# Graph layers in fp32: the states of 33 units transposed by VectorE in blocks and rearranged by DMAs through DRAM, where TensorE transposed them

## The chip, the cores and the metric

One core of one Trainium2 chip. The metric is the device time of one execution in microseconds. The engines are named as the profile names them: PE (TensorE), ACT (ScalarE), DVE (VectorE), POOL (GpSimd) and SP (SyncE, which here issues DMAs only).

## The reference

Four graph layers work on x of shape (16, 512, 128) with one matrix adj of shape (512, 512). Each layer's output is added to its input and normalised over the last axis:

```python
x = _layernorm(x + L0(x, adj, weight, bias))              # (adj @ x + x) @ W + b, rows scaled to length 1
x = _layernorm(x + L1(x, adj, adj, w3.., u3.., w5.., 5))  # gated recurrence, five steps
x = _layernorm(x + L2(x, adj, W, b))                      # degree-normalised adj @ x, then W
x = _layernorm(x + L3(x, adj, W, e, bias))                # attention over adj: self and neighbour parts
```

One step of the recurrence L1, on a state h of shape (16, 512, 128):

```python
m = einsum('nm,bmd->bnd', adj, h)                  # both matrices are adj here
u3 = h @ u3_w.T + u3_b
av = concatenate([m, m], -1)
z = sigmoid(av @ w3_w.T + w3_b + u3)
r = sigmoid(av @ w4_w.T + w4_b + u3)
hv = tanh(av @ w5_w.T + w5_b + (r * h @ u5_w.T + u5_b))
h = (1 - z) * h + z * hv
```

## The kernel before, in words

**Units and slots.** One batch element in one layer or one recurrent step is a unit, so there are 16 x 8 = 128: units 0 to 15 are the first layer, 16 to 95 the five steps, 96 to 111 the third layer and 112 to 127 the last. Every engine runs the same loop over slots `s` (`for s in range(SLOTS): slot(s)`). In slot s the unit s is aggregated and earlier units are at later stages. Nothing but the order of instructions in each engine's `slot` and semaphores sets the order; there is no planner.

**Layouts.** Node 4p + t stands on partition p. A product with adj contracts over the nodes, so it wants a state with nodes on partitions: `nat_hi` and `nat_lo`. The element-wise work and the products with weights want features on partitions: `feat`, 128 x 512 per batch element. What DVE makes of a step is `feat`; for the next step it must be turned into `nat_*`.

**Two parts.** Products run on operands of a rounded type (fp32r). To keep fp32 precision each operand X is split into a high part and a low part X - high, and a product is three matmuls: high x high, high x low, low x high. An aggregation (L1061 to L1067) is 12 matmuls of 512 columns: four chunks of nodes, three products each, `nat_*` as the stationary operand (loaded by LDWEIGHTS) and adj as the moving one.

**PE in a slot of the recurrence.** 12 matmuls of the aggregation of unit s; 3 for the reset state of s - 2 into `cand_ps` (L1072); for u = s - 1 the gate product into `gate_ps[u % 2]`, 6 matmuls (L1085, L1087), and 3 of the candidate (L1089); then the transposes of `turns_at(s)`, for a state 4 of 128 x 128 in fp32 into `turn_ps` (L1103); and last 3 matmuls that add the difference of the update and the reset gate's weights to the same bank `gate_ps[u % 2]` (L1142), before which PE waits for `r_made`, ACT's sigmoid reading that bank (L493).

**ACT in a slot.** `gate_z` of s - 2 (L458), `agg_hi` of s (L476), tanh into `cand` of s - 2 (L486), the sigmoid `gate_r` of s - 1 (L493), `feat_hi` (L503), `reset_hi` (L512), and `nat_hi` of the state s - 4 from `turn_ps` (L518). In the outer layers it also squares rows (L527), seeds biases (L536), normalises (L441) and makes `nat_hi` from `res` (L432, L463, L540).

**DVE in a slot.** `agg_lo` (L817), three operations that end in the new state `feat` of s - 2 (L822, L826, L829), `gate_r` times the state of s - 1 (L834), `feat_lo` (L838), `reset_lo` (L843), and `nat_lo` of the state s - 4 from `turn_ps` (L848). In the outer layers statistics (L863, L867), sums (L777, L782) and `nat_lo` from `res` (L696, L877) stand there too.

**POOL** works on statistics only: it has nothing in the middle of the recurrence. **SP** issues all DMAs from one queue in the order written: loads, two copies of adj's parts, reloads of `later` at slots about 36 and 46, small transfers, and the stores of the results. `cand[u % 2]` alternates by unit: ACT's tanh of u overwrites that of u - 2.

**When a state is turned.** A state unit u (16 to 79) is finished by DVE in slot u + 2, transposed in slot u + 4 (`STATE_LAG`), and used as `nat_*` by the aggregation of slot u + 16. Slots 88 and 93 are the two slots of the recurrence, once all its stages are filled, in which `turns_at` is empty.

Of the kernel before, what the change touches and what calls it, by code (L numbers as in the profile page):

```python
# [22 lines left out]
P = 128  # L23
B, N, D = 16, 512, 128
# [148 lines left out]


def flat(v):
    return v.rearrange("p a n -> p (a n)")


def graph_layers(nc, x, adj, w0, b0, w3, b3, u3, ub3, w4, b4, w5, b5, u5, ub5, w2, b2, wl3, e, bl3, mix_dram, d_dram, out):
    with ExitStack() as ctx:  # L180
        def sb(name, shape, dt=F32):
            return ctx.enter_context(nc.sbuf_tensor(name, shape, dt))
# [158 lines left out]
        def _(sp):  # L341
# [77 lines left out]
        def _(act):  # L419
# [3 lines left out]
            for t in range(T):  # L423
                if t == T - 1:
                    act.wait_ge(x_in[0], 16)
                    act.activation(nat_hi[:, 0, :, :], res[:, 0, :, :], ACT.Copy).then_inc(x_hi_made, 1)
                act.wait_ge(eye_turned, t + 1)
                act.activation(eye_hi[:, :, t * P:(t + 1) * P], prep_ps[t][:, :].rearrange("p (k i) -> p k i", k=T),
                               ACT.Copy).then_inc(eye_hi_made, 1)
            for b in range(1, 3):  # L430
                act.wait_ge(x_in[b], 16)
                act.activation(nat_hi[:, b, :, :], res[:, b, :, :], ACT.Copy).then_inc(x_hi_made, 1)  # L432

# [12 lines left out]
            def slot(s):  # L446
# [13 lines left out]
                for n in norms_at(s, "split"):  # L460
                    if stage(n) != L3:
                        wait_normed(act, n)
                        act.activation(nat_hi[:, n % B, :, :], res[:, n % B, :, :], ACT.Copy).then_inc(split_hi_made, 1)  # L463
                for n in norms_at(s, "back"):
# [48 lines left out]
                u = s - STATE_LAG  # L513
                if is_inner(u):
                    k = TURN_NO["state", u]
                    act.wait_ge(turned, k + 1)
                    act.wait_ge(agg_done, u + 1)
                    act.activation(nat_hi[:, u % B, :, :], turn_ps[k % 2][:, :].rearrange("p (t d) -> p t d", t=T),  # L518
                                   ACT.Copy).then_inc(state_hi_made, 1)
# [18 lines left out]
                if s + 3 < B:  # L538
                    act.wait_ge(x_in[s + 3], 16)
                    act.activation(nat_hi[:, s + 3, :, :], res[:, s + 3, :, :], ACT.Copy).then_inc(x_hi_made, 1)  # L540
                if s == ADJ_AT:
# [45 lines left out]
        def _(pool):  # L587
# [23 lines left out]
            def slot(s):  # L611
# [15 lines left out]
                for n in norms_at(s, "stats"):  # L627
# [33 lines left out]
        def _(dve):  # L661
# [32 lines left out]
            def x_lo(b):  # L694
                dve.wait_ge(x_hi_made, b + 1)
                dve.tensor_tensor(nat_lo[:, b, :, :], res[:, b, :, :], nat_hi[:, b, :, :].bitcast(F32),  # L696
                                  ALU.subtract).then_inc(x_lo_made, 1)
# [14 lines left out]
            def slot(s):  # L712
# [132 lines left out]
                u = s - STATE_LAG  # L845
                if is_inner(u):
                    dve.wait_ge(state_hi_made, u - B + 1)
                    dve.tensor_tensor(nat_lo[:, u % B, :, :],  # L848
                                      turn_ps[TURN_NO["state", u] % 2][:, :].rearrange("p (t d) -> p t d", t=T),
                                      nat_hi[:, u % B, :, :].bitcast(F32), ALU.subtract).then_inc(turn_read, 1)  # L850
                for n in norms_at(s, "stats"):
# [22 lines left out]
                for n in norms_at(s, "split"):  # L874
                    if stage(n) != L3:
                        dve.wait_ge(split_hi_made, nth(SPLIT, n))
                        dve.tensor_tensor(nat_lo[:, n % B, :, :], res[:, n % B, :, :],  # L877
                                          nat_hi[:, n % B, :, :].bitcast(F32), ALU.subtract).then_inc(split_lo_made, 1)
                if s + 3 < B:
# [65 lines left out]
        def _(pe):  # L945
# [82 lines left out]
            def slot(s):  # L1028

                if s < UNITS:  # L1030
                    if s < B:
                        if s:
                            pe.wait_ge(x_lo_made, s + 1)
                    elif 2 * B <= s < AFTER:
                        pe.wait_ge(turn_read, reads(TURN_NO["state", s - B]))
                    else:
                        pe.wait_ge(split_lo_made, nth(SPLIT, s - B))
# [10 lines left out]
                    if s == 0:  # L1048
                        pe.wait_ge(eye_lo_made, 1)
                        pe.wait_ge(eye_hi_made, T)  # L1050
                        pe.wait_ge(x_hi_made, 1)
                        for k in range(T):
                            pe.matmul(ps, nat_hi[:, b, k, :], m_hi[:, k, :], start=(k == 0), stop=False)
                        pe.wait_ge(x_lo_made, 1)
                        for k in range(T):
                            pe.matmul(ps, nat_lo[:, b, k, :], m_hi[:, k, :], start=False, stop=False)
                        pe.wait_ge(eye_lo_made, T)
                        for k in range(T):
                            last = pe.matmul(ps, nat_hi[:, b, k, :], m_lo[:, k, :], start=False, stop=(k == T - 1))
                    else:  # L1060
                        for k in range(T):  # L1061
                            if s == AFTER + B:
                                pe.wait_ge(turn_read, reads(TURN_NO["mix", k]))
                            pe.matmul(ps, nat_hi[:, b, k, :], m_hi[:, k, :], start=(k == 0), stop=False)  # L1064
                            pe.matmul(ps, nat_hi[:, b, k, :], m_lo[:, k, :], start=False, stop=False)  # L1065
                            last = pe.matmul(ps, nat_lo[:, b, k, :], m_hi[:, k, :], start=False, stop=(k == T - 1))  # L1066
                    last.then_inc(agg_done, 1)  # L1067
# [102 lines left out]
```

## Time and profile before

| | |
|---|---|
| median of 3 runs | 760.96 us (760.62 to 761.38) |
| profiled execution, time / span | 760.57 us / 758.7 us |
| granted clock of PE | 0.998 |
| busy: PE, PE weight load | 747.5 us (99%), 626.9 us (83%) |
| busy: DVE, ACT, POOL | 638.1 us (84%), 503.1 us (66%), 159.4 us (21%) |
| DMA | 11612 packets, 17.21 MB |

The span is what the profiler recorded from the first to the last instruction; the execution's own time is a little longer. Busy time counts overlapping instructions once. Matmuls are pipelined: a row's duration is longer than the step from one start to the next, so PE's pace is read from the starts in the timeline, and a PE that is busy all the time can still be held up. On ACT and DVE too the recorded durations overlap somewhat. "PEld" is the weight load of PE. L numbers are lines of the kernel.

### The profile page before, as it was taken

The numbers are of one execution on the slowest core, as the hardware profiler recorded it, in microseconds if no ns is written. First come the engines' busy times: TensorE is split into PE (matmuls) and PEld (weight loads), VectorE is DVE, ScalarE is ACT, GpSimd is POOL, SyncE is SP. The second block draws the span as 40 slices with busy tenths as digits, with TensorE's granted clock in tenths as the row PEclk, the third lists the DMA queues.
The fourth block names the chain that finished last, engine by engine and source line by source line (L and its number), as shares of the span: only waits on it lengthen the run. The fifth ranks groups of instructions, "written<-read, shape, count | busy, mean of one in ns | idle before, by whom it ended". The sixth has DMA issues, their size and how long they took to land.

```text
span 758.7 us, 11706 instructions
## 1 busy us (share of the span) xinstructions
PE 747.5 (99%) x3768; PEld 626.9 (83%) x3768; DVE 638.1 (84%) x1473; ACT 503.1 (66%) x1047; POOL 159.4 (21%) x307
## 2 busy tenths in 40 slices
PE   8999999999999999999999999999999999999996
PEld 7888788888888888888888888888888888788886
DVE  5899998888888998877777788777999999787775
ACT  4899777666666676666666666666587858864433
POOL 1878420000000000000000000000122257654333
PEclk9999999999999999999999999999999999999999
DMA  6500000000031001000000000000000000101112
GB/s 213 221 1 2 1 1 1 1 1 1 0 119 15 0 2 56 1 0 1 1 1 0 1 2 0 1 1 1 0 1 1 1 0 2 26 4 42 57 43 84
DMA packets 11612, 17.21 MB, mean 23 GB/s; under 512 B 4512, under 2 KB 6048, under 8 KB 10912
## 3 DMA queue, kind: packets, MB, share of 16 engines
q1 hardware_dynamic: 11552, 16.47, 6.5%
q8 instruction: 31, 0.51, 0.3%
q14 instruction: 29, 0.24, 0.1%
HBM read 9.12 MB, written 5.25 MB: 19 GB/s over the span
## 4 chain that ended last, share of the span: by engine, by line
PE 80%; DVE 9%; ACT 6%; POOL 2%; issue 2%; DMA 1%; SPq 0%; POOLq 0%; ACTq 0%; DVEq 0%
PE agg_ps L1064 12%; PE agg_ps L1066 12%; PE agg_ps L1065 12%; PE gate_ps L973 6%; PE gate_ps L975 6%; PE gate_ps L974 6%; PE cand_ps L973 4%; PE cand_ps L975 4%; PE cand_ps L974 4%; PE turn_ps L1103 4%; PE gate_ps L980 3%; PE cand_ps L980 3%; DVE stats L863 1%; ACT res L441 1%; PE turn_ps L1107 1%
## 5 line engine op out<-in xcount | busy, mean ns | idle before, releaser
L1064 PE MATMUL agg_ps<-adj_hi,nat_hi 128*128 128x512 f32 x384 | 152.1, 396 | 0.0
L1066 PE MATMUL agg_ps<-adj_hi,nat_lo 128*128 128x512 f32 x384 | 150.2, 391 | 0.0
L1065 PE MATMUL agg_ps<-adj_lo,nat_hi 128*128 128x512 f32 x384 | 149.6, 390 | 0.0
L642 POOL TENSOR_SCALAR shift<-mean_var 128x4 f32<-128x4 f32 x62 | 24.5, 396 | 408.8 <-DVE mean_var L867 406.7
L817 DVE TENSOR_TENSOR agg_lo<-agg_ps,agg_hi 128x512 fp32r<-128x512 f32 x80 | 55.1, 689 | 57.5 <-ACT agg_hi L476 57.5
L512 ACT ACTIVATE reset_hi<-gate_r 128x512 fp32r<-128x512 f32 x80 | 50.6, 633 | 78.1 <-DVE gate_r L834 78.1
L493 ACT ACTIVATE gate_r<-gate_ps,bias 128x512 f32<-128x512 f32 x80 | 55.2, 690 | 48.4 <-PE gate_ps L975 48.4
L1066 PEld LDWEIGHTS agg_ps<-adj_hi,nat_lo 128*128 128x128 f32 x384 | 72.1, 188 | 16.2
L1065 PEld LDWEIGHTS agg_ps<-adj_lo,nat_hi 128*128 128x128 f32 x384 | 72.2, 188 | 15.6
L1064 PEld LDWEIGHTS agg_ps<-adj_hi,nat_hi 128*128 128x128 f32 x384 | 72.1, 188 | 15.1
L476 ACT ACTIVATE agg_hi<-agg_ps 128x512 fp32r<-128x512 f32 x80 | 48.7, 608 | 44.0 <-PE agg_ps L1066 43.7
L644 POOL TENSOR_TENSOR rstd<-mean_var,half 128x4 f32<-128x4 f32 x62 | 69.2, 1116 | 5.2
L973 PE MATMUL gate_ps<-agg_hi,w_hi 128*128 128x512 f32 x160 | 69.5, 434 | 0.6 <-ACT gate_r L493 0.4
L975 PE MATMUL gate_ps<-agg_lo,w_hi 128*128 128x512 f32 x160 | 62.8, 393 | 0.0
L974 PE MATMUL gate_ps<-agg_hi,w_lo 128*128 128x512 f32 x160 | 62.7, 392 | 0.0
L843 DVE TENSOR_TENSOR reset_lo<-gate_r,reset_hi 128x512 fp32r<-128x512 f32 x80 | 55.4, 693 | 8.4 <-ACT reset_hi L512 0.7
L822 DVE TENSOR_TENSOR cand<-cand,feat 128x512 f32<-128x512 f32 x80 | 55.2, 690 | 4.6
L486 ACT ACTIVATE cand<-cand_ps,bias 128x512 f32<-128x512 f32 x80 | 55.2, 691 | 5.6
L826 DVE TENSOR_TENSOR cand<-cand,gate_z 128x512 f32<-128x512 f32 x80 | 55.4, 692 | 2.7
L829 DVE TENSOR_TENSOR feat<-feat,cand 128x512 f32<-128x512 f32 x80 | 55.3, 692 | 2.7
L838 DVE TENSOR_TENSOR feat_lo<-feat,feat_hi 128x512 fp32r<-128x512 f32 x80 | 54.7, 684 | 0.0
L834 DVE TENSOR_TENSOR gate_r<-gate_r,feat 128x512 f32<-128x512 f32 x80 | 54.7, 683 | 0.0
(205 smaller groups left out, 1753.8 us busy)
## 6 DMA issues: line engine op xcount, KB each, us to landing
res<-in_x SPq DMA_DIRECT2D x16, 256.0 KB, 5.7
out<-res SPq DMA_DIRECT2D x16, 256.0 KB, 2.0
rows<-in_adj SPq DMA_DIRECT2D x4, 256.0 KB, 3.9
adj_hi<-eye_hi SPq DMA_DIRECT2D x1, 1024.0 KB, 9.9
adj_lo<-eye_lo SPq DMA_DIRECT2D x1, 1024.0 KB, 11.7
later<-in_adj SPq DMA_DIRECT2D x1, 1024.0 KB, 6.4
mix_rows<-mix SPq DMA_DIRECT2D x1, 1024.0 KB, 7.9
later<-mix_rows SPq DMA_DIRECT2D x1, 1024.0 KB, 4.7
```

Source lines behind the costliest of these rows:

```text
L486: act.activation(cand[:, u % 2, :], cand_ps[u % 2][:, :], ACT.Tanh, bias=bias[:, B_H:B_H + 1]).then_inc(cand_made, 1)
L493: act.activation(gate_r[:, u % 2, :], gate_ps[u % 2][:, :], ACT.Sigmoid, bias=bias[:, B_R:B_R + 1]).then_inc(r_made, 1)
L644: pool.tensor_tensor(rstd[:, i % RING, :], r, half[:, :], ALU.pow).then_inc(rstd_made, 1)
L826: dve.tensor_tensor(cand[:, u % 2, :], cand[:, u % 2, :], gate_z[:, u % 2, :], ALU.mult).then_inc(move_made, 1)
L829: dve.tensor_tensor(feat[:, u % B, :], feat[:, u % B, :], cand[:, u % 2, :], ALU.add).then_inc(state_made, 1)
L843: dve.tensor_tensor(reset_lo[:, :], gate_r[:, u % 2, :], reset_hi[:, :].bitcast(F32), ALU.subtract).then_inc(reset_lo_made, 1)
L973: pe.matmul(ps, w_hi[:, w, :], hi, start=start, stop=False, skip_group_check=True)
L974: pe.matmul(ps, w_lo[:, w, :], hi, start=False, stop=False, skip_group_check=True)
L975: return pe.matmul(ps, w_hi[:, w, :], lo, start=False, stop=stop, skip_group_check=True)
L1064: pe.matmul(ps, nat_hi[:, b, k, :], m_hi[:, k, :], start=(k == 0), stop=False)
L1065: pe.matmul(ps, nat_hi[:, b, k, :], m_lo[:, k, :], start=False, stop=False)
L1066: last = pe.matmul(ps, nat_lo[:, b, k, :], m_hi[:, k, :], start=False, stop=(k == T - 1))
```

## The change

For the 33 units 45 to 77 (`BY_DMA`) PE no longer transposes the state. DVE transposes the 16 blocks of 32 x 32 of `feat` in each of the four chunks and writes them into `cand[u % 2]`, which is free by then. SP stores that to DRAM (`state_blocks`) with four DMAs of 32 partitions and, one unit later, reads it back with four DMAs, which put each block into its place in `nat_lo`, whole values for the moment. ACT rounds them into `nat_hi` in slot u + 5 (before: from `turn_ps` in slot u + 4), and POOL subtracts that in place, so that `nat_lo` holds the low parts. ACT's tanh of a unit two later now waits for the store to be done.

So that a DMA writes runs of 128 words, `nat_hi` and `nat_lo` change from [chunk, feature] to [feature, chunk] per partition. That holds for all 128 units: every weight load of an aggregation reads 128 words with a step of four words (16 bytes), and ACT and DVE write `nat_*` with this step where a unit isn't moved by DMA (`by_chunk`). The other 31 state units and the outer layers are otherwise as before. `PARTED` gives the order in which ACT makes the high parts.

```diff
+BY_DMA = range(45, 78)
+BLOCK = 32
+BLOCKS = P // BLOCK
...
-    if is_inner(s - STATE_LAG):
+    if is_inner(s - STATE_LAG) and s - STATE_LAG not in BY_DMA:
         found.append(("state", s - STATE_LAG))
...
+SWAP_LAG = 5
+PARTED = sorted((u for u in range(B, LAST)), key=lambda u: (u + (SWAP_LAG if u in BY_DMA else STATE_LAG), u in BY_DMA))
+def swaps(u):
+    return 16 * BLOCKS * sum(v <= u and v % 2 == u % 2 for v in BY_DMA)
...
+def by_chunk(v):
+    return v.rearrange("p d t -> p t d")
...
-        nat_hi = sb("nat_hi", [P, B, T, D], F32R)
-        nat_lo = sb("nat_lo", [P, B, T, D], F32R)
+        nat_hi = sb("nat_hi", [P, B, D, T], F32R)
+        nat_lo = sb("nat_lo", [P, B, D, T], F32R)
...
+            def swap_back(u):
+                sp.wait_ge(swap_out[u % 2], swaps(u))
+                if u - 2 in BY_DMA:
+                    sp.wait_ge(swap_in[u % 2], swaps(u - 2))
+                rows_of = swap_dram[u % B].rearrange("(a i) (q c) -> q i a c", a=BLOCKS, q=BLOCKS)
+                for q in range(BLOCKS):
+                    sp.dma_start(nat_lo[q * BLOCK:(q + 1) * BLOCK, u % B].rearrange("i (a d) k -> i a (d k)", a=BLOCKS).bitcast(F32),
+                                 rows_of[q]).then_inc(swap_in[u % 2], 16)
+            for u in BY_DMA:
+                sp.wait_ge(swapped, nth(BY_DMA, u))
+                for a in range(BLOCKS):
+                    cut = slice(a * BLOCK, (a + 1) * BLOCK)
+                    sp.dma_start(swap_dram[u % B, cut, :], cand[cut, u % 2, :]).then_inc(swap_out[u % 2], 16)
+                if u - 1 in BY_DMA:
+                    swap_back(u - 1)
+            swap_back(BY_DMA[-1])
...
-                    act.activation(nat_hi[:, 0, :, :], res[:, 0, :, :], ACT.Copy).then_inc(x_hi_made, 1)
+                    act.activation(by_chunk(nat_hi[:, 0]), res[:, 0, :, :], ACT.Copy).then_inc(x_hi_made, 1)
...
-                    if u >= B + 2:
+                    if u - 2 in BY_DMA:
+                        act.wait_ge(swap_out[u % 2], swaps(u - 2))
+                    elif u >= B + 2:
                         act.wait_ge(state_made, u - B - 1)
                     act.activation(cand[:, u % 2, :], cand_ps[u % 2][:, :], ACT.Tanh,
...
+                u = s - SWAP_LAG
+                if u in BY_DMA:
+                    act.wait_ge(swap_in[u % 2], swaps(u))
+                    act.activation(flat(nat_hi[:, u % B]), flat(nat_lo[:, u % B]).bitcast(F32),
                                    ACT.Copy).then_inc(state_hi_made, 1)
...
+                u = s - SWAP_LAG
+                if u in BY_DMA:
+                    pool.wait_ge(state_hi_made, nth(PARTED, u))
+                    if is_step(s - 2):
+                        pool.wait_ge(state_made, s - 2 - B + 1)
+                    pool.tensor_tensor(flat(nat_lo[:, u % B]), flat(nat_lo[:, u % B]).bitcast(F32),
+                                       flat(nat_hi[:, u % B]).bitcast(F32), ALU.subtract).then_inc(swap_lo_made, 1)
...
-                if is_inner(u):
-                    dve.wait_ge(state_hi_made, u - B + 1)
-                    dve.tensor_tensor(nat_lo[:, u % B, :, :],
+                if is_inner(u) and u not in BY_DMA:
+                    dve.wait_ge(state_hi_made, nth(PARTED, u))
+                    dve.tensor_tensor(by_chunk(nat_lo[:, u % B]),
...
+                u = s - 2
+                if u in BY_DMA:
+                    dve.wait_ge(state_made, u - B + 1)
+                    dve.transpose(cand[:, u % 2, :].rearrange("p (q d k) -> p k q d", q=BLOCKS, k=T),
+                                  feat[:, u % B, :].rearrange("p (k q i) -> p k q i", q=BLOCKS, k=T)).then_inc(swapped, 1)
...
-                        pe.wait_ge(turn_read, reads(TURN_NO["state", s - B]))
+                        if s - B in BY_DMA:
+                            pe.wait_ge(swap_lo_made, nth(BY_DMA, s - B))
+                        else:
+                            pe.wait_ge(turn_read, reads(TURN_NO["state", s - B]))
...
-                            pe.matmul(ps, nat_hi[:, b, k, :], m_hi[:, k, :], start=(k == 0), stop=False)
+                            pe.matmul(ps, nat_hi[:, b, :, k], m_hi[:, k, :], start=(k == 0), stop=False)
```

## Rows read from the trace of the kernel before

**Rows 1.** The page's chain that ended last, by engine, whole span.
```profile
PE 80%; DVE 9%; ACT 6%; POOL 2%; issue 2%; DMA 1%; SPq 0%; POOLq 0%; ACTq 0%; DVEq 0%
```

**Rows 2.** Waits, 250 to 450 us: waiter, releaser, us in total, times, longest us.
```profile
DVE agg_lo L817 <- ACT agg_hi L476: 27.9, 27, 1.1
```

**Rows 3.** Timeline of PE, slots 57, 58: start us, us, engine, line, operation.
```profile
355.72 0.39 PE L973 MATMUL cand_ps<-reset_hi,w_hi 128*128 128x512 f32 x1
...
358.21 0.39 PE L975 MATMUL cand_ps<-agg_lo,w_hi 128*128 128x512 f32 x1
358.44 0.60 PE L1103 MATMUL turn_ps<-ident,feat 128*128 128x128 f32 x4
358.79 0.48 PE L973 MATMUL gate_ps<-agg_hi,w_hi 128*128 128x512 f32 x1
359.11 0.39 PE L974 MATMUL gate_ps<-agg_hi,w_lo 128*128 128x512 f32 x1
```

**Rows 4.** Timeline of ACT, the reset gate's sigmoid in slots 57, 58 and 59.
```profile
351.34 0.69 ACT L493 ACTIVATE gate_r<-gate_ps,bias 128x512 f32<-128x512 f32 x1 [0.67 <-PE gate_ps L975]
...
357.96 0.69 ACT L493 ACTIVATE gate_r<-gate_ps,bias 128x512 f32<-128x512 f32 x1 [0.67 <-PE gate_ps L975]
...
364.55 0.69 ACT L493 ACTIVATE gate_r<-gate_ps,bias 128x512 f32<-128x512 f32 x1 [0.67 <-PE gate_ps L975]
```

**Rows 5.** Timeline of PE in slot 88, which has no transposes.
```profile
556.31 0.39 PE L975 MATMUL cand_ps<-agg_lo,w_hi 128*128 128x512 f32 x1
556.80 0.50 PE L973 MATMUL gate_ps<-agg_hi,w_hi 128*128 128x512 f32 x1
557.13 0.40 PE L974 MATMUL gate_ps<-agg_hi,w_lo 128*128 128x512 f32 x1
```

**Rows 6.** Timeline of ACT, the reset gate's sigmoid in slots 88 and 89.
```profile
556.06 0.69 ACT L493 ACTIVATE gate_r<-gate_ps,bias 128x512 f32<-128x512 f32 x1 [0.67 <-PE gate_ps L975]
...
562.57 0.69 ACT L493 ACTIVATE gate_r<-gate_ps,bias 128x512 f32<-128x512 f32 x1 [0.67 <-PE gate_ps L975]
```

**Rows 7.** Weight loads, by line (ns min/median/max); by form (us, mean ns); PE's timeline.
```profile
L1110 PEld LDWEIGHTS turn_ps<-ident,rows x4: 197/209/212, 46.3 to 46.6; 128*128 128x128 f32 x4
L1103 PEld LDWEIGHTS turn_ps<-ident,feat x320: 138/139/153, 103.1 to 648.3; 128*128 128x128 f32 x160
L980 PEld LDWEIGHTS gate_ps<-w_all,agg_all 128*128 128x128 f32 x64 | 8.4, 191 | 0.6
46.37 0.64 PE L1110 MATMUL turn_ps<-ident,rows 128*128 128x128 f32 x4
```

**Rows 8.** Windows: length, then busy us (count) by engine, clock, DMA share, GB/s.
```profile
40.00:80.00 40.00, 39.95 (x235) 34.78 (x234) 37.10 (x150) 40.00 (x144) 31.72 (x55) 1.00 0.01 1
560.00:600.00 40.00, 39.90 (x186) 32.47 (x185) 38.27 (x90) 31.81 (x62) 11.69 (x20) 1.00 0.00 1
```

**Rows 9.** Timeline of ACT in slot 12, its two high parts.
```profile
57.44 0.88 ACT L540 ACTIVATE nat_hi<-res 128x512 fp32r<-128x512 f32 x1
57.96 0.87 ACT L463 ACTIVATE nat_hi<-res 128x512 fp32r<-128x512 f32 x1
```

**Rows 10.** Lines of ACT, 40 to 80 us: busy us, mean ns, idle before.
```profile
L463 ACT ACTIVATE nat_hi<-res 128x512 fp32r<-128x512 f32 x10 | 9.0, 897 | 0.0
```

**Rows 11.** Timeline of DVE, the end of slot 57 and the start of slot 58.
```profile
354.15 0.69 DVE L843 TENSOR_TENSOR reset_lo<-gate_r,reset_hi 128x512 fp32r<-128x512 f32 x1
354.76 0.68 DVE L848 TENSOR_TENSOR nat_lo<-turn_ps,nat_hi 128x512 fp32r<-128x512 f32 x1
356.55 0.69 DVE L817 TENSOR_TENSOR agg_lo<-agg_ps,agg_hi 128x512 fp32r<-128x512 f32 x1 [1.10 <-ACT agg_hi L476]
```

**Rows 12.** POOL's two-input operation of 128x128 (ns min/median/max).
```profile
L616 POOL TENSOR_TENSOR cand<-gate_z x3: 467/788/1938, 17.7 to 20.6; 128x128 f32<-128x128 f32 x3
```

**Rows 13.** SP's timeline, and DMA issues: count, KB each, median us to landing.
```profile
13.94 2.40 SPq L349 DMA_DIRECT2D res<-in_x  x5
out<-res SPq DMA_DIRECT2D x16, 256.0 KB, 2.0
d_cols_row<-row_d SPq DMA_DIRECT2D x1, 2.0 KB, 8.7
```

More of the change, by code:

```diff
@@ L172, in nth, with graph_layers @@
     return order.index(u) + 1
+def by_chunk(v):
+    return v.rearrange("p d t -> p t d")
 def flat(v):
     return v.rearrange("p a n -> p (a n)")
-def graph_layers(nc, x, adj, w0, b0, w3, b3, u3, ub3, w4, b4, w5, b5, u5, ub5, w2, b2, wl3, e, bl3, mix_dram, d_dram, out):
+def graph_layers(nc, x, adj, w0, b0, w3, b3, u3, ub3, w4, b4, w5, b5, u5, ub5, w2, b2, wl3, e, bl3, mix_dram, d_dram, swap_dram, out):
     with ExitStack() as ctx:
@@ L308, in graph_layers @@
         turned = sem("turned")
+        swapped, swap_lo_made = sem("swapped"), sem("swap_lo_made")
+        swap_out, swap_in = ([sem(f"{n}{i}") for i in range(2)] for n in ("swap_out", "swap_in"))
         turn_read, turn_read_act, rows_read = sem("turn_read"), sem("turn_read_act"), sem("rows_read")
@@ L431, in _ @@
                 act.wait_ge(x_in[b], 16)
-                act.activation(nat_hi[:, b, :, :], res[:, b, :, :], ACT.Copy).then_inc(x_hi_made, 1)
+                act.activation(by_chunk(nat_hi[:, b]), res[:, b, :, :], ACT.Copy).then_inc(x_hi_made, 1)
             def norm(n, first, end):
@@ L462, in slot @@
                         wait_normed(act, n)
-                        act.activation(nat_hi[:, n % B, :, :], res[:, n % B, :, :], ACT.Copy).then_inc(split_hi_made, 1)
+                        act.activation(by_chunk(nat_hi[:, n % B]), res[:, n % B, :, :], ACT.Copy).then_inc(split_hi_made, 1)
                 for n in norms_at(s, "back"):
@@ L539, in slot @@
                     act.wait_ge(x_in[s + 3], 16)
-                    act.activation(nat_hi[:, s + 3, :, :], res[:, s + 3, :, :], ACT.Copy).then_inc(x_hi_made, 1)
+                    act.activation(by_chunk(nat_hi[:, s + 3]), res[:, s + 3, :, :], ACT.Copy).then_inc(x_hi_made, 1)
                 if s == ADJ_AT:
@@ L695, in x_lo @@
                 dve.wait_ge(x_hi_made, b + 1)
-                dve.tensor_tensor(nat_lo[:, b, :, :], res[:, b, :, :], nat_hi[:, b, :, :].bitcast(F32),
+                dve.tensor_tensor(by_chunk(nat_lo[:, b]), res[:, b, :, :], by_chunk(nat_hi[:, b]).bitcast(F32),
                                   ALU.subtract).then_inc(x_lo_made, 1)
@@ L876, in slot @@
                         dve.wait_ge(split_hi_made, nth(SPLIT, n))
-                        dve.tensor_tensor(nat_lo[:, n % B, :, :], res[:, n % B, :, :],
-                                          nat_hi[:, n % B, :, :].bitcast(F32), ALU.subtract).then_inc(split_lo_made, 1)
+                        dve.tensor_tensor(by_chunk(nat_lo[:, n % B]), res[:, n % B, :, :],
+                                          by_chunk(nat_hi[:, n % B]).bitcast(F32), ALU.subtract).then_inc(split_lo_made, 1)
                 if s + 3 < B:
@@ L1052, in slot @@
                         for k in range(T):
-                            pe.matmul(ps, nat_hi[:, b, k, :], m_hi[:, k, :], start=(k == 0), stop=False)
+                            pe.matmul(ps, nat_hi[:, b, :, k], m_hi[:, k, :], start=(k == 0), stop=False)
                         pe.wait_ge(x_lo_made, 1)
                         for k in range(T):
-                            pe.matmul(ps, nat_lo[:, b, k, :], m_hi[:, k, :], start=False, stop=False)
+                            pe.matmul(ps, nat_lo[:, b, :, k], m_hi[:, k, :], start=False, stop=False)
                         pe.wait_ge(eye_lo_made, T)
                         for k in range(T):
-                            last = pe.matmul(ps, nat_hi[:, b, k, :], m_lo[:, k, :], start=False, stop=(k == T - 1))
+                            last = pe.matmul(ps, nat_hi[:, b, :, k], m_lo[:, k, :], start=False, stop=(k == T - 1))
                     else:
@@ L1063, in slot @@
                                 pe.wait_ge(turn_read, reads(TURN_NO["mix", k]))
-                            pe.matmul(ps, nat_hi[:, b, k, :], m_hi[:, k, :], start=(k == 0), stop=False)
-                            pe.matmul(ps, nat_hi[:, b, k, :], m_lo[:, k, :], start=False, stop=False)
-                            last = pe.matmul(ps, nat_lo[:, b, k, :], m_hi[:, k, :], start=False, stop=(k == T - 1))
+                            pe.matmul(ps, nat_hi[:, b, :, k], m_hi[:, k, :], start=(k == 0), stop=False)
+                            pe.matmul(ps, nat_hi[:, b, :, k], m_lo[:, k, :], start=False, stop=False)
+                            last = pe.matmul(ps, nat_lo[:, b, :, k], m_hi[:, k, :], start=False, stop=(k == T - 1))
                     last.then_inc(agg_done, 1)
@@ L1165 @@
     args.append(nc.dram_tensor("d_cols_row", (1, N), F32, kind="Internal").ap())
+    args.append(nc.dram_tensor("state_blocks", (B, P, N), F32, kind="Internal").ap())
     args.append(nc.dram_tensor("out", (B, N, D), F32, kind="ExternalOutput").ap())
```

7 lines of the change are left out of this document (4 added, 3 removed).

## The prediction

> **What bounds the kernel now.** I read the chain of waits by engine first: 80% of the chain that ended last is PE work [rows 1]. The list of waits for 250 to 450 us names no wait of PE at all; the longest of DVE is for ACT's agg_hi, 1.1 us at a time [rows 2]. So in the recurrent stage PE never stands still, and a slot (one unit's aggregation with the gate and candidate products of the units before it) is the sum of its matmuls. The timeline of PE in one slot shows their pace: a 512-column matmul starts 0.227 us after the one before (its 0.39 us is mostly overlap), and the four transposes of a state take 0.35 us plus a slow restart: 358.21 for the last candidate product, 358.44 the first transpose, 358.79 the first product of the update gate, 359.11 the next one [rows 3]. Without transposes and restart those two products would come 0.227 and 0.454 after 358.21; the second comes at 0.90. The transposes cost 0.44 us a slot by this count. A slot is (364.55 - 351.34)/2 = 6.605 us by the starts of the reset gate's sigmoid [rows 4].
>
> **What taking them out is worth.** The change takes the transposes out of 33 slots (units 45 to 77, slots 49 to 81). At 0.44 us that would be 14.5 us. But what stands behind them in PE's queue is the update gate's product, which goes into the same PSUM bank gate_ps and so waits until ACT has read the reset gate (r_made). That sigmoid starts at 357.96 and lasts 0.69 us, to 358.65 [rows 4]; PE's candidate products are issued by 358.44. So most of the 0.44 us is a wait that the transposes now cover. The trace holds the case itself: slot 88 (and 93) has nothing to transpose. There the last candidate product starts at 556.31, the next product at 556.80, 0.05 us after the sigmoid's end (556.06 + 0.69), and the one after at 557.13 [rows 5, 6]: 0.82 us for two products, against 0.90 with transposes. From sigmoid to sigmoid this slot lasts 562.57 - 556.06 = 6.51 us [rows 6], against 6.605 [rows 4]. It is worth 0.09 us a slot (0.07 to 0.10 by the two readings and their rounding), 33 x 0.09 = 3.0 us. The chain gate product, sigmoid, update product does not depend on which slots are neighbours, so I take it for consecutive slots too.
>
> **What is added on DVE.** nat_lo (0.68 us) goes from 33 slots; a 32x32 block transpose of 128x512 comes in at the same place in the slot. The trace has no such instruction; the nearest rows are DVE's 0.68 to 0.69 us at this size, the bounds are 0.35 (half) and 1.37 us (twice). DVE now ends its slot at 354.76 + 0.68 = 355.44 and starts the next at 356.55 [rows 11], 1.1 us idle, 1.0 us in the shorter slot. A transpose of up to 1.7 us is covered by that; nothing waits for it but a DMA. I take 0.7 us and no cost. In slots 47 and 48 both stand, 0.7 us more, still under 1.1.
>
> **POOL.** The low part moves to POOL: 128x512, two inputs in SBUF. POOL's 128x128 took 0.467 us at its shortest [rows 12]; four times that, 1.87 us, is the upper end for 512 columns, 0.47 the lower, and I take 1.3. It is released by ACT's nat_hi, which comes after reset_hi, when DVE's reset_lo (354.15 + 0.69) is running [rows 11]. From then DVE has the transpose (one input), its idle time and agg_lo (one input in PSUM); the next DVE instruction with two SBUF inputs follows agg_lo, at about 357.3, 2.4 us after reset_lo. POOL has nothing else in slots 50 to 82, and PE needs the part eleven slots later. Cost 0.
> POOL and DVE do seem to hinder each other: the same POOL operation took 1.938 and 0.788 us where DVE was busy [rows 12]. The Trainium skill ("SBUF — State Buffer", Who interferes with whom) says that a DVE instruction with two SBUF inputs and a GpSimd one that reads SBUF exclude each other for a whole instruction; this placement meets that only at the end of reset_lo, so its rule changes a chance below and not the sum.
>
> **DMAs.** Per unit four writes of 64 KB in 2 KB rows and four reads in 512-byte runs, all from SP. Five issues took 2.40 us [rows 13], so about 0.48 us each: 8 x 0.48 = 3.8 us of a 6.5 us slot. With DVE's transpose ending at T, the writes are issued by T + 1.9 and landed by T + 3.9 (2.0 us for a store of 2 KB rows; 8.7, which a store of single words took, is the upper end [rows 13]). The tanh that overwrites cand two units later comes about 1.2 + 6.5 = 7.7 us after T. The reads of the unit before go out next, from T + 1.9 to T + 3.8, land by T + 6 to T + 9 and are wanted by nat_hi about 1.8 slots after T, T + 11.6. Both covered. The wait in SP's queue for `later` (slot 46) is over before the first unit's turn, and what follows the loop is wanted after slot 100. ACT's nat_hi becomes an SBUF copy, 0.62 for 0.58 us, with 0.7 us idle in the slot.
>
> **What changes for every unit: 16-byte strides.** nat_hi and nat_lo become [D, T], so each of the 1,536 aggregation loads reads every fourth word, and ACT and DVE write (DVE also reads) with that stride wherever a state isn't moved by DMA.
> PE: the trace has strided loads (L1110, turning rows of adj): 0.209 against 0.139 us recorded, and four such transposes take 0.64 in all against 0.60 for dense ones [rows 3, 7]: (0.64 - 0.284)/3 = 0.119 against (0.60 - 0.272)/3 = 0.109 us from one to the next. So a strided load needs 0.12 us, inside the 0.227 of a 512-column matmul. Dense loads of 0.19 us recorded keep the same 0.109 pace (L980) [rows 7], so it isn't the recorded length that counts. What is left is the first load after short matmuls, in 46 slots of the outer layers: 46 x 0.011 = 0.5 us lost. Bounds: 0, and 1,536 x (0.188 + 0.070 - 0.227) = 48 us if the whole recorded length had to fit.
> ACT: between 40 and 80 us it is busy all 40.0 us [rows 8], ten nat_hi of L463 [rows 10] and five of L540 stand there, 0.52 us from one to the next [rows 9]. There any extra goes straight into the end of the first layer. Lower bound 0; by the strided load's pace (0.119/128 = 0.93 ns an element, against ACT's 0.52/512 = 1.02 ns) nothing to little; by its recorded length (half again) 0.26 us each; by twice the time 0.52. I take 0.02, the pace being what the engine delivers: 15 x 0.02 = 0.3 us. DVE, at 0.6 us for 512 (1.17 ns an element), the same way 0.
>
> **Sum.** -3.0 + 0.5 + 0.3 = -2.2 us. The profiled execution took 760.57 us around its span of 758.7, 0.39 below the median of 760.96. 760.57 - 2.2 = 758.4; on the median's level 758.8 us.
>
> **Rivals.**
> (B) A strided write costs ACT and DVE time. In its favour: half again in the recorded length of strided loads; against: their pace, and that both engines need over 1 ns an element anyway. Place: ACT between 40 and 80 us, where 15 nat_hi cost 0.26 to 0.52 us each, 3.9 to 7.8 us; and DVE between 560 and 600 us, busy 38.27 of 40 [rows 8], where six nat_lo, one a slot, at +0.3 to +0.6 need 1.8 to 3.6 us and find 1.7: 0.1 to 1.9. In the recurrent slots idle time covers both. 758.8 - 0.3 + 4.0 to + 9.7 = 762.5 to 768, middle 765. It turns the sign from 0.15 us for each nat_hi. The Trainium skill ("Advanced Engine Details and Errata", SBUF Cachelines) holds for this: SBUF has 16-byte lines, at least two hits on one are needed to hide its latency, and a new line for each element pays; the strided load's 0.209 us agrees with it, its pace hardly. Chance 0.24.
> (C) POOL and DVE block each other after all, as 1.938 us for 0.467 shows they can: if the low part (1.3 us) delays reset_lo, PE's product of the reset state, which starts at 355.72 [rows 3], is late by 1.3 less the 0.8 us since reset_lo's end at 354.84 [rows 11], 0.5 x 33 = 17 us: 776. Against: the order above. 0.05.
> (D) The strided weight load holds up each matmul: up to 48 us, say 780. Against: the pace. 0.04.
> (E) The DRAM stores land late (8.7 us): T + 1.9 + 8.7 is 2.9 us past the tanh's turn, once in two slots: 48 us, 806. Against: 2.0 us for like stores. 0.05.
> (F) The full 0.44 us comes free: 746.5. Against: slot 88. 0.04.
>
> **Numbers.** The forecast has 0.58, its own range 757.6 to 760. A change under 0.2% (1.5 us) can't be told from none. Within the forecast 0.42 lie over 0.2% faster, 0.15 within, 0.01 above; B gives 0.02 to no change and 0.22 to slower; C and D 0.09 slower; E 0.04 slower and 0.01 none; F 0.04 faster. Faster 0.46, same 0.18, slower 0.36. Range 757.6 to 767: it leaves out F, C, D, E and the top of B, about 0.2.
>
> **What would show it.** Slots 49 to 81 of 6.51 us from sigmoid to sigmoid, with the first update-gate product 0.05 us behind the sigmoid's end; a new wait of PE for gate_r, some 0.3 us in each of 33 slots. Aggregation matmuls still 0.227 us apart and their loads near 0.25 us: if they are wider apart, D. nat_hi of L463 and L540 at a step of 0.52 us, and the first sigmoid of the recurrent stage where it was: if it is 4 us or more later, B. DVE idle 1 us before agg_lo, and diff not delayed: else C. A wait of ACT's tanh for a DMA: E. The prediction is wrong if slots 49 to 81 aren't 0.07 to 0.10 us shorter, or if the other slots lose more than about 1 us together.

## The result, and the profile after

The kernel after takes 792.53 us (791.67 to 793.84, 4 runs), before 761.17 (4 runs beside them): ratio 1.041, interval 1.0397 to 1.0423, slower by 31.4 us. The forecast was 758.8 us with a range of 757.6 to 767. It was wrong, and on the wrong side.

The page after, its busy time by engine and its chain by engine (before: [rows 1]):

```profile
PE 766.4 (97%) x3636; PEld 688.8 (87%) x3636; DVE 690.4 (87%) x1473; ACT 539.6 (68%) x1047; POOL 227.1 (29%) x340
...
PE 50%; DVE 26%; ACT 16%; issue 5%; POOL 1%; DMA 1%; SPq 0%; ACTq 0%; POOLq 0%; DVEq 0%
```

PE's share of the chain went from 80% to 50%, DVE's from 9% to 26%, ACT's from 6% to 16%. With 132 matmuls fewer PE is busy 19 us longer, its weight loads 62 us. The main groups of instructions that touch nat_hi or nat_lo, and the block transpose, by line and shape (count, then busy us, mean ns, idle before):

```profile
L1125 PEld LDWEIGHTS agg_ps<-adj_lo,nat_hi 128*128 128x128 f32 x384 | 119.2, 311 | 0.0
L501 ACT ACTIVATE nat_hi<-res 128x512 fp32r<-128x512 f32 x48 | 56.4, 1180 | 3.7 <-DVE res L863 3.7
L934 DVE TENSOR_TENSOR nat_lo<-res,nat_hi 128x512 fp32r<-128x512 f32 x48 | 51.8, 1081 | 0.0
L697 POOL TENSOR_TENSOR nat_lo<-nat_lo,nat_hi 128x512 fp32r<-128x512 f32 x33 | 42.9, 1300 | 252.2 <-ACT nat_hi L563 252.2
L906 DVE STREAM_TRANSPOSE cand<-feat 128x512 f32<-128x512 f32 x33 | 36.6, 1110 | 0.0
L900 DVE TENSOR_TENSOR nat_lo<-turn_ps,nat_hi 128x512 fp32r<-128x512 f32 x31 | 34.0, 1097 | 9.3 <-ACT nat_hi L558 9.3
L558 ACT ACTIVATE nat_hi<-turn_ps 128x512 fp32r<-128x512 f32 x31 | 33.7, 1087 | 0.0
L563 ACT ACTIVATE nat_hi<-nat_lo 128x512 fp32r<-128x512 f32 x33 | 20.4, 618 | 0.0
```

The same load and the same high part in the trace of before:

```profile
L1065 PEld LDWEIGHTS agg_ps<-adj_lo,nat_hi 128*128 128x128 f32 x384 | 72.2, 188 | 15.6
L518 ACT ACTIVATE nat_hi<-turn_ps 128x512 fp32r<-128x512 f32 x64 | 37.1, 580 | 0.0
```

Whatever has the 16-byte step takes longer: the weight load 311 ns for 188, ACT's high part 1.09 for 0.58 us (L558), DVE's low part 1.10 for 0.68 us (L900; before in [rows 11]). What is dense in the new route is as forecast: ACT's copy 0.618, POOL's part 1.300 us.

In slots 49 to 81 the predicted wait is there (list of waits, 330 to 520 us: waiter, releaser, us in total, times, longest), and the timelines of PE and ACT show it:

```profile
PEld gate_ps L1030 <- ACT gate_r L533: 15.2, 29, 0.5
```

```profile
406.60 0.39 PE L1032 MATMUL cand_ps<-agg_lo,w_hi 128*128 128x512 f32 x1
407.09 0.50 PE L1030 MATMUL gate_ps<-agg_hi,w_hi 128*128 128x512 f32 x1
407.43 0.40 PE L1031 MATMUL gate_ps<-agg_hi,w_lo 128*128 128x512 f32 x1
```

```profile
399.72 0.69 ACT L533 ACTIVATE gate_r<-gate_ps,bias 128x512 f32<-128x512 f32 x1 [0.68 <-PE gate_ps L1032]
...
406.35 0.69 ACT L533 ACTIVATE gate_r<-gate_ps,bias 128x512 f32<-128x512 f32 x1 [0.68 <-PE gate_ps L1032]
```

The update product starts at 407.09, 0.05 us after the sigmoid's end, as in slot 88 before [rows 5]. Yet from sigmoid to sigmoid it is 6.63 us, not 6.51: more than the 6.605 of before [rows 4]. The stalls in the first layer read like this (busy us by engine as in [rows 8], 40 to 80 us):

```profile
40.00:80.00 40.00, 35.31 (x197) 33.39 (x196) 38.22 (x135) 40.00 (x117) 31.29 (x49) 1.00 0.01 1
```

Before, PE ran 235 matmuls in this window and ACT 144 instructions [rows 8]; now 197 and 117, with ACT again busy all 40 us. PE is held back by ACT. ACT's pace there, from one high part to the next, is 0.91 us where it was 0.52 [rows 9]:

```profile
61.15 1.23 ACT L585 ACTIVATE nat_hi<-res 128x512 fp32r<-128x512 f32 x1
62.06 1.28 ACT L501 ACTIVATE nat_hi<-res 128x512 fp32r<-128x512 f32 x1
```

How the difference spreads, from the starts of the aggregations in the traces (us against the trace of before; each column adds up a stretch of slots; runs of the next section stand below it). Each row is one profiled execution, so its sum need not be the difference of the medians:

```
slots                    0-8   9-16  17-22  23-35  36-48  49-81  82-96  97-112   113-126
after                    3.5    7.5    2.9    1.7    5.0    1.3    2.9     4.9       2.3
layout_only              2.0    7.5    2.9    1.8    5.0    3.0    3.0     4.8       2.3
pe_stride_only           1.6    1.0   -0.8    1.3    1.2    3.0    1.2     1.0       2.3
write_stride_only        1.5    7.3    3.1    0.8    4.9    0.0    2.4     3.5       0.0
act_stride_only          0.3    7.1    2.6    0.2    1.8    0.0    1.5     0.1       0.0
dve_write_stride_only    0.3    2.1    1.4    0.0    0.5    0.0    0.6     3.9       0.0
dve_read_stride_only     0.5    3.9    1.6    0.0    1.1    0.0    1.0     5.0       0.0
no_turn                  0.0    0.0    0.0    0.0    0.0   -3.0    0.0     0.0       0.0
dense_route              0.1    0.0    0.0    0.0    0.0   -3.0    0.0     0.0       0.0
dense_route_late         0.0    0.0    0.0    0.0    0.0  -16.6    0.7     0.0       0.0
before_late              0.0    0.0    0.0    0.0    0.0   -0.8    0.8     0.3       0.0
dense_wide_late          0.0    0.1   -0.8    0.1   -0.1  -15.8   -1.5     1.5       0.0
```

Three of these traces hold stretches in which PE's granted clock fell to half, the level of 1.2 GHz (windows: length, busy us by engine, clock, DMA share, GB/s; the traces of after, of dve_write_stride_only and, two rows, of dve_read_stride_only):

```profile
12.00:14.00 2.00, 2.00 (x6) 1.57 (x5) 1.35 (x2) 0.00 (x0) 0.00 (x0) 0.50 0.27 76
```

```profile
656.00:658.00 2.00, 2.00 (x7) 1.61 (x6) 1.74 (x5) 1.41 (x4) 1.67 (x5) 0.50 0.00 0
```

```profile
56.00:58.00 2.00, 2.00 (x6) 1.52 (x6) 1.97 (x9) 2.00 (x5) 1.67 (x2) 0.50 0.00 0
660.00:662.00 2.00, 2.00 (x10) 1.81 (x9) 1.89 (x9) 2.00 (x6) 1.81 (x3) 0.50 0.00 0
```

In the second stretch products of 512 columns start 0.43 us apart:

```profile
657.00 0.63 PE L1135 MATMUL agg_ps<-eye_hi,nat_lo 128*128 128x512 f32 x1
657.43 0.63 PE L1133 MATMUL agg_ps<-eye_hi,nat_hi 128*128 128x512 f32 x1
```

Ahead of these stretches PE had stood idle: 1.84 us before the one at 656 us, 2.45 before the one at 56, 1.29 before that of after. (In layout_only 1.35 us of idleness at about 9 us brought no fall, so idleness alone doesn't tell.) The fall adds about 1.8 us to slots 97 to 112 of dve_write_stride_only: that much is lost in slots 105 and 106, where write_stride_only, with more strided accesses, lost nothing, and the traced execution took 769.48 us, the other three 767.36 to 767.90. It adds about 1.6 us to slots 9 to 16 and some 2 us to slots 97 to 112 of dve_read_stride_only. It also goes with the 1.5 us that after has more than layout_only in slots 0 to 8.

### The profile page after: what moved, and what is told of

It reads as the page before. It is cut to its first block, busy times and chain, and to the rows that moved or that the text cites. A ratio compares the mean times of both kernels' runs of the same rounds, so it can differ in the third digit from the quotient of the medians.

```text
span 791.4 us, 11737 instructions
## 1 busy us (share of the span) xinstructions
PE 766.4 (97%) x3636; PEld 688.8 (87%) x3636; DVE 690.4 (87%) x1473; ACT 539.6 (68%) x1047; POOL 227.1 (29%) x340
## 4 chain that ended last, share of the span: by engine, by line
PE 50%; DVE 26%; ACT 16%; issue 5%; POOL 1%; DMA 1%; SPq 0%; ACTq 0%; POOLq 0%; DVEq 0%
PE agg_ps L1124 9%; PE agg_ps L1125 8%; PE agg_ps L1126 8%; PE gate_ps L1030 5%; PE gate_ps L1032 4%; PE gate_ps L1031 4%; DVE cand L878 3%; DVE feat L881 3%; ACT gate_r L533 3%; DVE cand L874 3%; ACT nat_hi L558 3%; DVE gate_r L886 3%; DVE agg_lo L869 2%; PE gate_ps L1037 2%; DVE nat_lo L900 2%
## 5 line engine op out<-in xcount | busy, mean ns | idle before, releaser
L1124 PE MATMUL agg_ps<-adj_hi,nat_hi 128*128 128x512 f32 x384 | 156.2, 407 | 0.0
L1125 PE MATMUL agg_ps<-adj_lo,nat_hi 128*128 128x512 f32 x384 | 152.6, 398 | 0.0
L1126 PE MATMUL agg_ps<-adj_hi,nat_lo 128*128 128x512 f32 x384 | 152.1, 396 | 0.0
L1124 PEld LDWEIGHTS agg_ps<-adj_hi,nat_hi 128*128 128x128 f32 x384 | 118.8, 309 | 3.6
L1125 PEld LDWEIGHTS agg_ps<-adj_lo,nat_hi 128*128 128x128 f32 x384 | 119.2, 311 | 0.0
L1126 PEld LDWEIGHTS agg_ps<-adj_hi,nat_lo 128*128 128x128 f32 x384 | 118.9, 310 | 0.0
L697 POOL TENSOR_TENSOR nat_lo<-nat_lo,nat_hi 128x512 fp32r<-128x512 f32 x33 | 42.9, 1300 | 252.2 <-ACT nat_hi L563 252.2
L687 POOL TENSOR_SCALAR shift<-mean_var 128x4 f32<-128x4 f32 x62 | 37.2, 601 | 129.5 <-DVE mean_var L924 127.1
L501 ACT ACTIVATE nat_hi<-res 128x512 fp32r<-128x512 f32 x48 | 56.4, 1180 | 3.7 <-DVE res L863 3.7
```

Of the source, the lines that this page charges most:

```text
L1124: pe.matmul(ps, nat_hi[:, b, :, k], m_hi[:, k, :], start=(k == 0), stop=False)
L1125: pe.matmul(ps, nat_hi[:, b, :, k], m_lo[:, k, :], start=False, stop=False)
L1126: last = pe.matmul(ps, nat_lo[:, b, :, k], m_hi[:, k, :], start=False, stop=(k == T - 1))
```

## The experiments

Theory S: the strides make the whole loss; the new route is covered and gives back only what the wait for the sigmoid leaves. Rival M: the new route itself (block transpose, DMAs, POOL's part) costs most of it. The medians of before beside the three sets of runs were 761.10, 760.78 and 761.29 us.

**Layout only.**

```diff
-BY_DMA = range(45, 78)
+BY_DMA = range(0)
-            swap_back(BY_DMA[-1])
```

> The kernel after with no unit moved by DMA: all states are transposed by PE, and only the layout [feature, chunk] of nat_hi and nat_lo with its 16-byte steps is left. Theory S (the strides make the whole loss): slots 49 to 81 lose what the missing transposes gave back there, 33 x 0.07 = 2.2 us, so 792.5 + 2.2 = 794.7, 793 to 797. Rival M (the block transposes, DMAs and GpSimd part cost most of the 31 us): under 775. Rival N (neither alone, the two together): 775 to 790.

793.57 us, ratio 1.0429 (1.0414 to 1.0445): +32.5. Without a single DMA, block transpose or POOL part of the new route the loss is there whole. M falls.

**PE's strided loads alone.** The four views of a unit's 512 words:

```diff
-pe.matmul(ps, nat_hi[:, b, k, :], ...)
+pe.matmul(ps, strided(nat_hi[:, b], k), ...)   # flat(v).rearrange("p (d t) -> p d t", t=T)[:, :, k]
```

> The kernel before, except that the aggregation's weight loads read every fourth word of a unit's 512 (they read the wrong words; everything else is as before, ACT and DVE write densely). Theory S1, from the trace of after: each of 1,536 loads takes 0.31 for 0.188 us and the 512-column matmuls start 0.232 to 0.236 apart instead of 0.227, some 0.09 us in each of 80 slots of the recurrence and 0.16 in 47 outer slots, 15 us: 776, 772 to 779. Rival S2 (the longer steps of after are a consequence of late operands and not of the loads): within 1 us of before. My prediction's own reading of the strided loads gave +0.5 us: 761.6.

772.88 us, 1.0156 (1.014 to 1.0171): +11.8. PE's timeline in the middle of the recurrence:

```profile
400.40 0.40 PE L1069 MATMUL agg_ps<-adj_hi,nat_hi 128*128 128x512 f32 x1
400.64 0.39 PE L1070 MATMUL agg_ps<-adj_lo,nat_hi 128*128 128x512 f32 x1
400.88 0.40 PE L1071 MATMUL agg_ps<-adj_hi,nat_lo 128*128 128x512 f32 x1
401.11 0.40 PE L1069 MATMUL agg_ps<-adj_hi,nat_hi 128*128 128x512 f32 x1
```

Three steps take 0.71 us, 0.237 each, where 0.227 stood. Over the trace the median step behind a strided load is 235 or 236 ns. By the table 3.0 us in 33 slots, 0.09 a slot; in the last layer 2.3/14 = 0.16, since there the first load after short matmuls is exposed: in slot 118 the second product starts 0.435 us after the first, before 0.314.

**ACT's and DVE's accesses alone, and each by itself.**

```diff
# write_stride_only: layout_only, and PE's views
-nat_hi[:, b, :, k]
+dense(nat_hi[:, b], k)                          # flat(v)[:, k * P:(k + 1) * P]
# act_stride_only: of these only ACT's writes of nat_hi with the step
# dve_write_stride_only: only DVE's writes of nat_lo; dve_read_stride_only: only its reads of nat_hi
```

> The layout-only kernel, except that the aggregation's weight loads read 128 words in a row (the wrong words), so that only ACT's and DVE's writes, and DVE's reads of nat_hi, have 16-byte steps. Theory S1: 794.7 - 15 = 780, 776 to 784, because these accesses take 1.09 to 1.18 us on ACT and 1.1 us on DVE where they took 0.58 to 0.69, and the first layer and the last step of the recurrence have no idle time for it. Rival S2 (the loads matter not at all): 794.7. Rival W (ACT and DVE hide it all): 761.5.

> The kernel before, except that ACT writes nat_hi with 16-byte steps for all units (DVE and PE read it and write densely, so the values are misplaced). The writes of ACT and the accesses of DVE together cost 23.9 us. Theory A (ACT is full between 40 and 80 us and each write takes 0.5 us more there; DVE's part counts in the last step of the recurrence and where the L2 matrix is prepared): ACT alone 10 to 14 us, 771 to 775. Rival D (DVE is the one that counts): under 767. Rival AA (ACT alone makes it all): 783 or more.

> The kernel before, except that DVE writes nat_lo with 16-byte steps for all units (ACT writes and DVE and PE read densely, so the low parts are misplaced). ACT and DVE together cost 23.9 us, ACT's writes alone 14.1. Theory A (the write port is slowed by the step: nat_lo takes 1.1 us for 0.68): some 10 us, 771, 768 to 773, by the remaining 9.8 us. Rival R (on DVE it is the strided read of nat_hi that made 1.1 us): nat_lo stays at 0.68 us and the time within 1 us of before.

> The kernel before, except that DVE reads nat_hi with 16-byte steps where it makes nat_lo; all writes and PE's reads are dense. Theory A: the instruction takes 0.68 us as before and the time is 761 if reads are free, as the strided loads' pace had made me think. Rival R: 1.1 us and about 770.

Together 784.96 us, 1.0314 (1.0297 to 1.0332): +23.9, 1 us above the expected range. ACT alone 774.92, 1.019 (1.0176 to 1.0204): +14.1. DVE's writes alone 767.73, 1.0088 (1.0073 to 1.0103): +6.4, less than the 10 expected. DVE's reads alone 773.82: +12.5, in one execution, which had two stretches at half clock. Without their 3.6 us the reads would cost about 9 us, an estimate. The instructions, by line (ACT alone, then writes alone, then reads alone):

```profile
L567 ACT ACTIVATE nat_hi<-turn_ps 128x512 fp32r<-128x512 f32 x64 | 68.7, 1073 | 0.0
```

```profile
L909 DVE TENSOR_TENSOR nat_lo<-turn_ps,nat_hi 128x512 fp32r<-128x512 f32 x64 | 68.4, 1069 | 0.0
```

```profile
L909 DVE TENSOR_TENSOR nat_lo<-turn_ps,nat_hi 128x512 fp32r<-128x512 f32 x64 | 67.8, 1059 | 0.0
```

Of the two DVE runs the first bore out its theory in the instruction's length (the rival's 0.68 us fell), the second its rival (the theory's free read fell): a strided write and a strided read each bring DVE's recorded length to 1.06 or 1.07 us, and both together only to 1.10. The step from nat_lo to the next instruction where DVE is full tells them apart better. Before it was 0.58 to 0.61 us; it is about 0.90 with the write and 0.98 with the read (the lines below, in this order), and 1.00 with both in layout_only, so that behind a strided read the strided write adds next to nothing:

```profile
637.70 1.07 DVE L943 TENSOR_TENSOR nat_lo<-res,nat_hi 128x512 fp32r<-128x512 f32 x1
638.60 0.76 DVE L865 TENSOR_TENSOR gate_ps<-res,bias_rows 128x512 f32<-128x512 f32 x1
```

```profile
636.32 1.05 DVE L943 TENSOR_TENSOR nat_lo<-res,nat_hi 128x512 fp32r<-128x512 f32 x1
637.30 0.68 DVE L843 TENSOR_TENSOR res<-turn_ps,res 128x512 f32<-128x512 f32 x1
```

This speaks for the read costing more than the write; the time of the single execution with reads alone doesn't show it by itself.
The parts measured alone, 11.8 + 23.9 = 35.7 us, overlap by 3.2 us in the 32.5 of layout_only.

**What leaving the transposes out can give.**

```diff
+LEFT_OUT = range(45, 78)      # no turn, no high and low part, no wait for them
```

> The kernel before without the transposes of units 45 to 77, without their high and low parts on ACT and DVE and without the wait for them: their nat_hi and nat_lo keep older contents. This is what the change could save at most if nothing came in its place. Theory R (the update product's wait for the reset gate's sigmoid takes the place of the transposes): 33 x 0.07 to 0.10 us = 2.3 to 3.3 us, 758.5, with slots of 6.51 to 6.54 us. Rival F (PE saves the transposes whole): 33 x 0.44 = 14.5 us, 746.5, slots of 6.16 us.

757.89 us, 0.9958 (0.9943 to 0.9973): -3.2. Rival F (the full 0.44 us a slot comes free) falls for this order of PE's work. The wait in its trace (330 to 500 us) is that of the kernel after:

```profile
PEld gate_ps L975 <- ACT gate_r L495: 13.6, 26, 0.5
```

**The route without the strides.** Layout as before, DVE's blocks in dense rows, the stores put 128-byte runs into place:

```diff
-dve.transpose(cand[:, u % 2, :].rearrange("p (q d k) -> p k q d", q=BLOCKS, k=T),
+dve.transpose(cand[:, u % 2, :].rearrange("p (q k d) -> p k q d", q=BLOCKS, k=T),
-sp.dma_start(swap_dram[u % B, cut, :], cand[cut, u % 2, :])
+sp.dma_start(swap_dram[u % B].rearrange("p n -> (p n)").rearrange("(i m a d) -> a i m d", i=BLOCK, m=BLOCKS * T, a=BLOCKS)[a],
+             cand[cut, u % 2, :].rearrange("i (m d) -> i m d", d=BLOCK))
-rows_of = swap_dram[u % B].rearrange("(a i) (q c) -> q i a c", a=BLOCKS, q=BLOCKS)
+rows_of = swap_dram[u % B].rearrange("(i q) n -> q i n", q=BLOCKS)
```

> The kernel after with the layout of before, [chunk, feature], for all units: DVE transposes the blocks of the same 33 units into dense rows, the stores put runs of 32 words (128 bytes) into place in DRAM, and the readback is rows of 2 KB. Theory S+R (the strides are the whole loss; without them what remains is the saving that the wait for the sigmoid leaves): as without the transposes, 761.1 - 3.2 = 757.9, 757 to 759.5. Rival M (the route itself costs: the block transpose, the small DMA packets or GpSimd's part hold something up): 761 or more; if the stores land too late for the tanh, a wait of ACT for a DMA in slots 49 to 81 and 780 or more.

757.47 us, 0.9956 (0.9942 to 0.9969), the time of no_turn: the route is wholly covered. The block transpose by line, and the two DMAs (KB, median us to landing):

```profile
L907 DVE STREAM_TRANSPOSE cand<-feat 128x512 f32<-128x512 f32 x33 | 23.2, 705 | 0.0
```

```profile
state_blocks<-cand SPq DMA_DIRECT2D x132, 64.0 KB, 2.2
nat_lo<-state_blocks SPq DMA_DIRECT2D x132, 64.0 KB, 2.1
```

**The update product later.** In slots 49 to 81 it goes behind the first three matmuls of the next aggregation:

```diff
-                if is_step(u):
+                if is_step(u) and s not in LATE_Z:
                     (the update product of u)
...
                             last = pe.matmul(ps, nat_lo[:, b, k, :], m_hi[:, k, :], ...)
+                            if k == 0 and s - 1 in LATE_Z:
+                                update(s - 2)
```

> The dense route, and in slots 49 to 81 PE issues the update gate's product (3 matmuls) not at the end of the slot but after the first 3 matmuls of the next slot's aggregation. Theory R (the sigmoid of the reset gate, not PE's work, ends slots 49 to 81): PE has something to do while it waits, slots of 27 x 0.227 = 6.13 to 6.2 us, 33 x 0.37 = 12 us below the dense route, 745.5; if DVE, whose seven operations and block transpose need about 6.0 us (5.96 in the kernel after), becomes the bound instead, 33 x 0.25 = 8 us below, 749.5. Rival (the wait isn't what ends these slots): no gain on the dense route.

> The kernel before without the transposes and the high and low parts of units 45 to 77 (older contents stay), as before in no_turn, and with the update gate's product moved behind the first 3 matmuls of the next aggregation in slots 49 to 81. Theory R: the whole 0.44 us of the transposes and some of the restart come free, 33 x 0.44 to 0.47 = 14.5 to 15.5 us, 746. Rival: 757.9 as without the move.

> The kernel before, all transposes kept, with the update gate's product moved behind the first 3 matmuls of the next aggregation in slots 49 to 81. Theory R: the transposes already fill the wait for the sigmoid, so little is left: a slot is 27 x 0.227 + 0.44 = 6.57 instead of 6.605 us, 33 x 0.03 = 1.1 us faster, 760. Rival (the late product alone made the 13 us of the dense route with it): 748.

dense_route_late 744.55 us, 0.9786 (0.9773 to 0.9799); no_turn_late 744.61, 0.9787 (0.9774 to 0.98); before_late 761.26, 0.9998 (0.9989 to 1.0008). The PE timeline of dense_route_late:

```profile
402.88 0.39 PE L1034 MATMUL cand_ps<-agg_lo,w_hi 128*128 128x512 f32 x1
403.10 0.39 PE L1131 MATMUL agg_ps<-adj_hi,nat_hi 128*128 128x512 f32 x1
403.33 0.39 PE L1132 MATMUL agg_ps<-adj_lo,nat_hi 128*128 128x512 f32 x1
403.56 0.39 PE L1133 MATMUL agg_ps<-adj_hi,nat_lo 128*128 128x512 f32 x1
403.78 0.39 PE L1032 MATMUL gate_ps<-agg_hi,w_hi 128*128 128x512 f32 x1
```

No gap is left. By the table these 33 slots give 16.6 us, 0.50 each: the transposes' 0.44 and the slow restarts. The late product alone gives nothing measurable, where 1.1 us was expected (0.8 us in slots 49 to 81, lost again in slots 82 to 96), and the missing transposes alone 3.2: only both together give 16. DVE did not become the bound; it still waits in each slot of 330 to 500 us:

```profile
DVE agg_lo L871 <- ACT agg_hi L516: 17.6, 28, 1.2
```

**Wider.** 35 units (45 to 79), the late product in slots 18 to 96.

```diff
-BY_DMA = range(45, 78)
+BY_DMA = range(45, 80)
-LATE_Z = range(49, 82)
+LATE_Z = range(18, 97)
```

> The dense route with the late update product for 35 units (45 to 79) instead of 33, and the late product in all slots 18 to 96. Theory R: two more slots at 6.13 for 6.605 us, 0.9 us, and 0.03 us in each of some 44 other slots, up to 1.3 us, less what DVE gives back in the last slots of the recurrence, where it is full: 742.5 to 744.5. Rival: the late product harms where the slot is ended by DVE or ACT (slots 18 to 23 and 88 to 96): above 744.6.

744.10 us (743.90 to 745.05), 0.9776 (0.9761 to 0.979). The interval overlaps that of dense_route_late, so that it is faster than that one isn't shown: by the table, what it gains in slots 17 to 22 and 82 to 96 is lost in 49 to 81 and 97 to 112. Against the kernel before both are faster by over 16 us.

## Why the prediction was wrong

- **Taking the transposes out, "33 x 0.09 = 3.0 us": right.** no_turn measured 3.2, and the mechanism is shown from both sides: with the update product moved, the same 33 slots give 16.6.
- **DVE's block transpose, POOL, DMAs, "no cost": right**, with one size off. The transpose took 1.11 us against the 0.7 taken, because it writes with the step; dense it takes 0.705. Idle time covered either. POOL 1.30 (1.3 taken), stores 1.7 us to landing (2.0 taken). C and E did not happen.
- **"What changes for every unit: 16-byte strides": the step that failed**, in all three of its readings.
  For PE I had 0.5 us; it is 11.8. I took the load of a 128-column transpose [rows 7] for the load of a 512-column product. That one took 0.209 us with the step, this one takes 0.311. The pace argument was half right: the matmul does not wait for the load's recorded end, or the step would be 0.31 us and the loss above D's 48 us. But the step isn't free: 0.227 becomes 0.235, 12 times a slot. Why it is 8 ns no run here tells. That the saving of slots 49 to 81 (0.09 us each) met a loss of 0.09 us from this alone is why they came out no shorter.
  For ACT I had 0.02 us an instruction; its step is 0.39 longer. I put the pace of PE's loads (0.93 ns an element) beside ACT's 1.02 and concluded that there was no room for a loss. The pace of one engine's reads said nothing of another's writes.
  For DVE I had nothing; its step is 0.3 us longer with the write, 0.4 with the read. ACT's and DVE's accesses together cost 23.9 us where the sum had 0.3.
- **Rival B was the right mechanism, with too few places.** It priced the two stretches that were full, 4.0 to 9.7 us in all, where 23.9 came. Of ACT's 14.1 us half, 7.1, fell in slots 9 to 16, within its 3.9 to 7.8; the rest in slots 17 to 22, in 36 to 48, where the third layer's matrix is prepared, and in 82 to 96. DVE's 0.1 to 1.9 held for its place, slots 82 to 96 (0.6 with the writes, 1.0 with the reads), but left out the first layer (2.1 with the writes) and slots 97 to 112 (also about 2.1, the table's 3.9 without what the half clock added). And B and D were kept apart as rivals, though one layout brings both: together they made 32.5 us, outside a range that ended just below B's top.
- The Trainium skill ("Advanced Engine Details and Errata", SBUF Cachelines) says that an access pays when each one falls on another 16-byte line, which I weighed against the pace of the strided load. The runs agree: one element per 16 bytes took ACT from 0.52 to 0.91 us a step and DVE from about 0.59 to 0.90 or 0.98. No other step was run, so the runs don't show that it is the line that counts, or from which step on.
- The Trainium skill ("SBUF — State Buffer", Who interferes with whom) says that a DVE instruction with two SBUF inputs contends with a GpSimd one that reads SBUF. That was hardly put to the test here: POOL's part overlapped reset_lo by at most 0.13 us, and reset_lo took 0.693 us on the page after as before.
- Left open: slots 49 to 81 take 6.64 us from aggregation to aggregation on average; no_turn's 6.51 and the loads' 0.09 make 6.60. The remaining 0.04 stands in small steps outside the aggregation (the first two products behind it start 0.237 and 0.236 us apart, in no_turn 0.227). Why isn't shown.

## What to carry to other kernels

A layout chosen so that one transfer is simple is paid by every other access to the tensor: here the DMAs of 33 units were made easy by a step that 1,536 weight loads, 95 writes of ACT and 95 of DVE then had to take. Price such a step per engine and per kind of access, add the prices up, and where the trace has no like row keep the factor of two inside the range.
Before work is taken off the busiest engine, look in the trace for a slot in which it is already missing; if the slot is hardly shorter, find the wait behind it and give the engine other work there. Either change alone was worth 3 us or nothing, the two together 16.

## What the runs showed of the hardware

- A weight load of 128 fp32 columns for an fp32r product took 188 ns dense and 311 ns with a 16-byte step, while that of a transpose took 139 and 209; the products of 512 columns behind it went from 227 to 235 ns a step.
- DVE's 32x32 block transpose of 128x512 in fp32 took 0.705 us with dense writes and 1.110 us with the step. A strided read together with a strided write took DVE 1.09 to 1.10 us in recorded length (nat_lo from PSUM), either alone 1.06 or 1.07, neither 0.68. The steps to the next instruction were about 1.00 us with both, 0.98 with the read, 0.90 with the write and 0.58 to 0.61 with neither.
- Stores of 64 KB into DRAM landed after 2.2 us in 128-byte runs and 1.7 us in 2 KB rows, four to a slot of 6.1 to 6.6 us.
- PE's granted clock fell to half (the level of 1.2 GHz) after PE had been idle for 1.84 us in one trace and 2.45 us in another. Products of 512 columns then started 0.43 us apart, and such a stretch cost 1.6 to 2 us.
